# A half pair's transposes moved right behind the next scores, and LayerNorm work of each chunk moved from VectorE to ScalarE, in a two-layer graph kernel

## What is computed

```python
h = relu(layernorm(x))
g = exp0(log0(h) @ embed);  g = h_add(g, embed_bias)            # hyperbolic maps: norm, tanh, arctanh
neigh = exp0(adj @ log0(g))
x = x + h_add(exp0(log0(concat(h, neigh)) @ layer), layer_bias)
h = relu(layernorm(x))
for beta in (beta1, beta2):                                     # two attention layers
    n = h / norm(h)
    s = where(adj > 0, beta * (n @ n.T), -1e9)
    h = leaky(softmax(s) @ h, 0.3)
x = x + h
```

## Time and profile before

| | us |
|---|---|
| median of 3 runs (lowest to highest) | 994.92 (993.46 to 997.03) |
| profiled execution | 993.61 |
| its span | 992.1 |
| PE busy | 935.3 (94%) |
| DVE busy | 819.4 (83%) |
| ACT busy | 511.4 (52%) |

### The profile page before, as it was taken

One profiled execution on the slowest core, in us unless ns is written; L12 is line 12 of the kernel. 1 busy time (PEld: TensorE's weight loads), 2 busy tenths in 40 slices (PEclk: granted clock), 3 DMA queues, 4 the chain that ended last, 5 costly groups with the idle time before them and its releaser, 6 DMA issues.

```text
span 992.1 us, 22921 instructions
## 1 busy us (share of the span) xinstructions
PE 935.3 (94%) x9024; PEld 698.0 (70%) x9024; DVE 819.4 (83%) x2110; ACT 511.4 (52%) x708; POOL 8.0 (1%) x21
## 2 busy tenths in 40 slices
PE   2789999999997989999999999989999999999996
PEld 1754444444444878788888888768878888888885
DVE  7791888888888987788988898988768788888887
ACT  2720211211216575765656677777565565656564
POOL 0000000000000000000000000000000000000000
PEclk9879999999998999999999999999999999999999
DMA  8219888888881444555555655535655556555630
GB/s 343 94 62 312 278 284 277 278 286 298 275 275 43 168 174 177 207 210 219 211 200 195 244 206 192 183 145 187 238 183 212 211 193 245 213 204 205 252 139 36
DMA packets 29971, 207.26 MB, mean 209 GB/s; under 512 B 3632, under 2 KB 4272, under 8 KB 5296
## 3 DMA queue, kind: packets, MB, share of 16 engines
q1 hardware_dynamic: 28224, 203.44, 56.6%
q0 software_dynamic: 640, 2.10, 0.5%
q10 hardware_dynamic: 1008, 0.33, 0.1%
HBM read 203.75 MB, written 2.10 MB: 207 GB/s over the span
## 4 chain that ended last, share of the span: by engine, by line
PE 84%; DVE 8%; ACT 4%; issue 2%; DMA 1%; DVEq 0%; POOL 0%; SPq 0%; POOLq 0%; ACTq 0%
PE acc_ps L463 20%; PE s_ps L614 17%; PE s_ps L600 10%; PE acc_ps L667 6%; PE acc_ps L663 6%; PE acc_ps L665 6%; PE acc_ps L644 5%; PE acc_ps L640 5%; PE acc_ps L642 5%; PE acc_ps L427 1%; DVE work L1604 1%; ACT work L971 1%; DMA x_sb<-in_x 1%; ACT set L764 1%; PE s_ps L441 1%
## 5 line engine op out<-in xcount | busy, mean ns | idle before, releaser
L971 ACT ACTIVATE work<-s_ps,beta_bias,beta_scale 128x1024 f32<-128x1024 f32 x144 | 173.5, 1205 | 223.2 <-PE s_ps L614 223.2
L463 PE MATMUL acc_ps<-ring,set 128*128 128x512 f32 x512 | 225.6, 600 | 3.1 <-DVE set L1230 3.1
L1622 DVE SCALAR_TENSOR_TENSOR h_all<-ring,s_ps 128x1024 f32<-128x1024 f32 x112 | 136.6, 1220 | 69.9 <-PE s_ps L600 69.1
L463 PEld LDWEIGHTS acc_ps<-ring,set 128*128 128x128 f32 x512 | 97.3, 192 | 120.8 <-issue 117.8
L1604 DVE TENSOR_TENSOR work<-work 128x1024 f16<-128x1024 f32 x96 | 132.5, 1380 | 5.4 <-ACT work L981 5.4
L981 ACT ACTIVATE work<-work 128x1024 f16<-128x1024 f32 x96 | 131.5, 1369 | 3.1
L1612 DVE SCALAR_TENSOR_TENSOR work<-ring,work 128x1024 f32<-128x1024 f32 x96 | 116.7, 1215 | 0.0
L614 PE MATMUL s_ps<-xt 128*128 128x512 f16 x432 | 107.6, 385 | 6.3 <-ACT work L971 5.5
L614 PE MATMUL s_ps<-set 128*128 128x512 f16 x432 | 105.3, 379 | 2.6 <-ACT t L1029 2.1
L663 PE MATMUL acc_ps<-set,work 128*128 128x129 f16 x576 | 103.5, 220 | 4.6 <-DVE accs L1639 2.7
L663 PE MATMUL acc_ps<-src,work 128*128 128x129 f16 x576 | 102.9, 219 | 1.9 <-ACT accs L995 1.9
(11 more groups left out here) (254 smaller groups left out, 1726.1 us busy)
## 6 DMA issues: line engine op xcount, KB each, us to landing
ring<-in_adj_t SPq DMA_DIRECT2D x192, 1024.0 KB, 5.0
x_sb<-in_x SPq DMA_DIRECT2D x4, 512.0 KB, 7.3
out<-x_sb POOLq DMA_DIRECT2D x8, 256.0 KB, 2.5
w<-in_layer ACTq DMA_DIRECT2D x2, 64.0 KB, 8.7
w<-in_embed ACTq DMA_DIRECT2D x1, 64.0 KB, 4.2
eb<-in_embed_bias ACTq DMA_DIRECT2D x1, 64.0 KB, 7.0
lb<-in_layer_bias ACTq DMA_DIRECT2D x1, 64.0 KB, 11.3
beta<-in_beta ACTq DMA_DIRECT2D x2, 0.5 KB, 14.6
```

The costliest lines, as they stand in the source:

```text
L463: last = nc.tensor.matmul(agg, v_sb[:, jb, :], ring[:, k, b, :], start=jb == 0, stop=jb == NB - 1)
L971: nc.scalar.activation(values[x.n % VR], score_ps, ACT.Exp, bias=beta_bias[:, x.la:x.la + 1], scale=beta_scale[:, x.la:x.la + 1]).then_inc ...
L1622: V.scalar_tensor_tensor(turned[x.off % MR].rearrange("p (b j) -> p b j", b=CB), ring[:, x.mir_tile % AR, :, ds(x.h * HB * P, HB * P)], 0. ...
```

## The change

Five things. SP waits for all of `x` before the first tile of `adj`. ACT's separate ReLU pass goes: PE transposes the normalised rows and ACT applies ReLU while copying out; the one-column products stand in the loop, four behind each group. In the aggregation, the squares of the product, the ReLU after LayerNorm with its squares, and the scaled rows move from DVE to ACT, as in the last chunk. The last chunk has 12 pauses instead of 11. In `pairs`, the transposes of half n-1 stand right behind scores(n), the mirrored sum is that of n-2, and DVE's slot runs low halves(n-1), row total, own mask(n-2), mirrored mask(n-1).

```diff
             for i in range(XP):
                 sp.dma_start(x_sb[...]).then_inc(x_in[i], 16)
+            sp.wait_ge(x_in[XP - 1], 16)
...
-            relu(0)
             for r in range(NC):
-                if r + 1 < NC:
-                    relu(r + 1)
                 act.wait_ge(ht_done, r + 1)
-                nc.scalar.activation(ht_sb[:, ds(r * CH, CH)], ht_ps[r % 2], ACT.Copy).then_inc(ht_copied, 1)
+                nc.scalar.activation(ht_sb[:, ds(r * CH, CH)], ht_ps[r % 2], ACT.Relu).then_inc(ht_copied, 1)
...
             # ACT, gnn_chunk
                 on(ACT.Tanh, sm(5, CB), sm(4, CB))
+                chunk_squares(dump)
                 log_terms(sm(4, CB), sm(5, CB), sm(6, CB))
                 if not first and not c_last(c):
                     split_columns(0, c - 1, xt_ps)
                 on(ACT.Tanh, sm(5, CB), sm(4, CB))
-                on(ACT.Copy, x_sb[:, ds(c * CB, CB), :], t1[:, :, :])
+                chunk_relu(c, dump)
+                chunk_rows(c)
...
+            def chunk_relu(c, unused):
+                asked_for()
+                for b in range(CB):
+                    last = nc.scalar.activation(t2[:, b, :], t1[:, b, :], ACT.Relu, bias=small[:, 3, b:b + 1])
+                last.then_inc(chunk_made, 1)
+                act.wait_ge(chunk_made, c * 2 + 1)
+                for b in range(CB):
+                    last = nc.scalar.activation(unused[:, b, :], t2[:, b, :], ACT.Square, accum_out=...)
+                last.then_inc(told, 1)
+                nc.scalar.activation(x_sb[:, ds(c * CB, CB), :], t1[:, :, :], ACT.Copy)
+            def chunk_rows(c):
+                asked_for()
...
+                    last = nc.scalar.activation(t2[:, b, :], t2[:, b, :], ACT.Copy, scale=small[:, 1, b:b + 1])
...
+                    last = nc.scalar.activation(t3[:, b, :], t2[:, b, :], ACT.Copy, scale=small[:, 9, b:b + 1])
+                last.then_inc(xn_ready[0], 1)
+                nc.scalar.activation(src[0][:, ds(c * CB, CB), F:2 * F], t2[:, :, :], ACT.Copy, scale=FS)
...
             # ACT, last_chunk
                 pause(-1)
+                pause(0)
                 on(ACT.Tanh, sm(5, CB), sm(4, CB))
                 split_columns(0, c - 1, xt_before_ps)
-                pause(0)
                 pause(1)
...
             # ACT, slot
-                x = at(n - 4)
-                if x and x.off is not None and x.h == 1 and x.a == 0:
+                i, x = row_ending.get(n - 4), at(n - 3)
+                first = x and x.off is not None and x.h == 1 and x.a == 0
+                if i is not None and rows_of[i].a == 0:
+                    first_total(i)
+                elif first:
                     first_flush(x)
                 if at(n):
                     raise_scores(at(n))
-                i = row_ending.get(n - 4)
-                if i is not None and rows_of[i].a == 0:
-                    first_total(i)
...
             # PE, pairs
                     if at(n):
                         pair_scores(at(n))
-                    done, fresh = at(n - 3), at(n - 1)
-                    if done and done.off is not None:
-                        mirrored_sum(done)
+                    done, turned_last, fresh = at(n - 3), at(n - 2), at(n - 1)
+                    if fresh and fresh.off is not None:
+                        turns(fresh)
+                    if turned_last and turned_last.off is not None:
+                        mirrored_sum(turned_last)
                     if done:
                         own_sum(done)
...
                     if n in turned_at:
                         columns_turned(n)
-                    if fresh and fresh.off is not None:
-                        turns(fresh)
...
             # DVE, slot
-                x = at(n - 4)
+                x = at(n - 3)
                 if x and x.off is not None and x.h == 1 and x.a:
                     flush(x)
+                if at(n - 1):
+                    low_halves(at(n - 1))
+                i = row_ending.get(n - 4)
+                if i is not None:
+                    row_total(i)
                 x = at(n - 2)
+                if x:
+                    own_mask(x)
+                x = at(n - 1)
                 if x and x.off is not None:
                     mirrored_mask(x)
...
```

More of the change, by code:

```diff
@@ L188, in build @@
         xs_ready = sem("xs_ready")
-        h_ready = sem("h_ready")
         web_made = sem("web_made")
@@ L423, in _ @@
                 last.then_inc(g_done, 1)
-            pe.wait_ge(web_made, 1)
-            for b in range(NB):
-                last = nc.tensor.matmul(gb_ps[:, b:b + 1], ht_sb[:, ts(b, P)], web[:, :], start=True, stop=True)
-            last.then_inc(gb_done, 1)
+                if r == 0:
+                    pe.wait_ge(web_made, 1)
+                for b in blocks(r):
+                    last = nc.tensor.matmul(gb_ps[:, b:b + 1], ht_sb[:, ts(b, P)], web[:, :], start=True, stop=True)
+                last.then_inc(gb_done, 1)
             pe.wait_ge(weights_in, 16 * 5)
@@ L1052, in slot @@
                     raise_scores(at(n))
-                i = row_ending.get(n - 4)
-                if i is not None and rows_of[i].a == 0:
-                    first_total(i)
+                if i is not None and first:
+                    first_flush(x)
                 if at(n):
@@ L1254, in gnn_chunk @@
                 w_in = w_last_ps if c_last(c) else w_ps
-                rows = ds(c * CB, CB)
-                both, squares = slice(CB, 2 * CB), small[:, 2, 0:2 * CB]
                 dve.wait_ge(w_done, c + 1)
@@ L1262, in gnn_chunk, with chunk_product @@
                     split_columns(0, c - 1, xt_before_ps)
+                chunk_product(w_in, c)
+                chunk_bias(c)
+                chunk_norms(c)
+                atanh_over(sm(2, CB), sm(0, CB), sm(1, CB), CB)
+                if not first and not c_last(c):
+                    split_columns(0, c - 1, xt_ps)
+                product_scalars(small[:, 0, both], sm(2, CB), sm(9, CB), sm(10, CB), y2[:, 1:2], CB)
+                chunk_sum()
+                chunk_stats(c)
+                chunk_deviations()
+                chunk_scales()
+                chunk_low(c)
+            both, squares = slice(CB, 2 * CB), small[:, 2, 0:2 * CB]
+            def chunk_product(w_in, c):
                 answered()
@@ L1311, in gnn_chunk, with chunk_deviations @@
[L1311 removed]
+                ask(V.tensor_scalar(sm(3, CB), mean_var[:, 0:CB, 0], -1.0, None, ALU.mult))
+            def chunk_deviations():
+                answered()
                 step(V.tensor_scalar(squares, squares, TINY, None, ALU.max))
                 inv_sqrt(sm(1, 2 * CB), squares, sm(3, 2 * CB))
[L1314 to L1316 removed]
```

210 lines of the change are left out of this document (70 added, 140 removed).

## The result

The changed kernel takes 1052.0 us (median of 4 runs, 1051.5 to 1054.8) against 994.2 before: ratio 1.0582, 95% interval 1.0553 to 1.0611. It is 58 us slower; the forecast was 1046, with a range of 1008 to 1066. The profiled execution has a span of 1050.0 us.

A forecast was written before the change was run, and what follows sets the result against it. PE was taken to bound aggregation and pairs. Terms -2.1 + 17.3 + 2 + 3 + 36 - 3.8 - 1.5 + 1.8 (column transposes) gave +52.7 on 993.6 us: 1046 us, range 1008 to 1066.

The forecast's parts named there:

- What bounds the kernel: Aggregation and pairs: PE alone sets the end, so taking work off DVE or ACT there gives nothing.
- The start: Before the aggregation: DVE's wait for one-column products goes and ACT loses a pass; -2.1 us, ends -3.5 and -1.
- The chunk chain: Aggregation: sum copies behind ACT's chunk work lengthen the period from 29.7 to 32.5 us; +17.3, ends 0 and 24.
- The clock: Aggregation: PE's idle times before layer products may lower its clock; +2 us, ends 0 and 8.4.
- The passage: From chunks to pairs: one more stall, as the last sum's copies stand behind chunk 6's rows; +3 us, ends 0 and +6.
- The row stalls: Pairs, row starts: PE waits for low halves 1.37, then 1.14 us, and later in rows; +36 us, ends 22 and 46.
- Waits that go: Pairs: PE's two 1.9 us waits for ACT's total of row 0 vanish; -3.8 us.
- The layer boundary: Between layers: the 2.12 us wait and the 1.4 of clock behind it may go; -1.5 us, ends -6 and 0.
- the row stalls would be absorbed: Rival, pairs: low halves come sooner, so only the chunks' longer period costs; 1010 us, chance 0.10.
- the chunk chain covered: Rival, aggregation: halves between stretch ACT's times, so the period stays 29.7 and the transition as before; 1024 us, chance 0.12.
- The faster case: Rival, everywhere: DVE early enough; chunk's chain ends 26.7 us after product, low halves 4.2 after scores began; 984 us, chance 0.07.
- The case in which each stall costs clock: Rival, chunks and pairs: six chunk stalls cost 8.4 us instead of 2, half the 1.37 waits another 8; 1061, chance 0.09.

The follow-up runs named there:

- copies between: The changed kernel, but ACT copies the next chunk's sum between this chunk's ReLU and its scaled rows: 1032.5 us, ratio 1.0367.
- chunks-only: The changed kernel with the old order of the pairs put back on PE, ACT and DVE: 1019.2 us, ratio 1.0236.
- start, total, row 5: The kernel before with the changed start, row 0's total ahead of ACT's exponential, and row 5's columns one step later: 984.5 us, ratio 0.9906.
- start only: The kernel before with the changed start alone: 990.4 us, ratio 0.9945.

## Why the prediction was right, and where its terms were not

**What bounds the kernel** held. PE bounds both long stages; DVE's 28 us less gave PE nothing in the aggregation, where the stage with copies between was as long as before. In the changed kernel it is no longer true there: ACT's and DVE's chain sets the period.

**The start** was put at -2.1. The profile shows -3.3, its first product with `adj` varies from 58.1 to 62.5 us among kernels with the same start, and timed alone the start is worth 5 us of median (990.4 against 995.3), beyond the end of -3.5 that I gave. Over the ten kernels with the new start the mark is at 60.4 on average, over the two with the old one at 62.8. The sign held; how good the size was stays open.

**The chunk chain** was right. Predicted were copies 29.5 us behind a product; they start 28.6 to 30.9 behind it. Predicted was a spacing of 32.5; it is 32.8 where the clock stayed full. The chain alone, at about 18 us by the estimate above, is what the 17.3 counted (six times the 2.8 of its text would be 16.8). PE's waits, 14.0 us in six, come out smaller because slower matmuls used up part of them. The term that was mis-sized is the next one.

**The clock** was put at +2 with ends 0 and 8.4; by the estimate above it cost about 7.6 in the aggregation, near the far end. I took the low value since waits of up to 1.9 had left the clock alone, but the new ones were 2.0 to 2.9. The Trainium skill, "TensorE: Matmul & The Clock Gate", section "HAM oscillation — how this bites in real kernels", describes a loop in which every tile starts cold behind its wait. The waits of its example are about 3 to 5 us, longer than these six, so my "by that rule all six chunks pay" went further than the Trainium skill does. The trace has the fall behind four of six waits (two stretches at 0.66, two at 0.50); directly behind the two of 2.06 the clock was full.

**The passage** is the step that failed. I priced the late last product at +3, and the chunks-only run shows 3.7, though not by that product alone. I priced the new order of the pairs there at nothing, and it costs 11.6. DVE makes the last chunk's rows between these halves and is the late engine. Before, PE had its two sums to do while low halves were late, since the transposes stood behind them; now they stand behind the transposes that wait. The run with the own sum ahead of the transposes gave 5.7 us of that back, the one with the transposes last 6.8. So this explains about half; which part of the new order makes the other half was not separated. I had counted what stands behind the waiting instruction only for row starts.

**The row stalls** were right in mechanism and place: PE waits for low halves at the first and second mirrored half of a row, and a third time in layer 1. The sizes were 36 in the sum against 23.9 measured. That the waits list as a whole has 35.9, as I had said it would, is luck: 12.0 of it stand in the passage, where I had put none. The first was 1.11 instead of 1.37: PE arrived later, since it counts from the end of the scores (1.46 behind their start, not 1.29), and the low halves came 0.09 sooner. The second was 0.52 instead of 1.14. There I added the lengths of DVE's instructions, but they overlap: low halves, total, reciprocal and the two masks start 1.19, 0.72, 0.09, 1.12 and 1.13 us apart, and the low halves end 9.69 us after the scores instead of 10.2. The third was 0.95 instead of 1.45, and in layer 2 there was hardly any. Row 1 of either layer has no second wait, where 0.45 was counted.

**Waits that go**: the 3.8 us were exact. The layer boundary gives more than 1.5 where the rest of the order is left alone.

**The rivals.** That the row stalls would be absorbed, or the chunk chain covered, fell: both waits are there. The faster case fell by both its conditions, as counted. The case in which each stall costs clock was half right: its chunk part (8.4) is near what happened, but the row stalls cost no clock, which reads 1.00 in the rest of the kernel before and after.

So the total came out within 6 us by a sum in which one term was 12 too low and another 11 too high. The direction and the two main mechanisms were shown by the runs; the closeness of the total was luck.

## What to carry to other kernels

An instruction that may wait is placed by what stands behind it on its engine: the new order of the pairs, in which two sums stand behind transposes that wait, cost 32 us, and with the own sum ahead of them and the row total first 20 came back. Before work is moved to an idle engine, look at what that engine does next and who waits for it: two copies of half a microsecond made the aggregation 25 us longer when they stood behind the moved work, and 0.1 when they stood between its parts. And when removing one wait changes nothing, look for a second that the first was hiding, and try both edits together.

## What had not been expected

In the start PE ran the same matmuls at about half speed for a longer or shorter time in kernels with the same start, and the first product with `adj` came at 58.1 to 62.5 us. Busy time by stretch (columns as above), first of the changed kernel, then with chunks only, which has the same start:

```profile
24.00:29.00 5.00, 5.00 (x49) 5.00 (x48) 4.93 (x35) 4.89 (x22) 0.00 (x0) 1.00 1.01 426
```

```profile
24.00:29.00 5.00, 5.00 (x25) 5.00 (x26) 4.93 (x37) 2.57 (x11) 0.00 (x0) 1.00 1.01 424
```

49 matmuls in five microseconds against 25, while the granted clock reads 1.00 in both; the rows don't say why, and no run shows that the clock does it, as two of my expectations had it. In this stretch 49, 47, 32 and 25 matmuls ran in four kernels with the same start (the changed one; start, total, row 5; start only; chunks only), and their first products with `adj` came in the same order: 58.1, 58.9, 60.6 and 62.5. It scatters every comparison of the start by up to 4 us.

Two waits of 2.06 us left the granted clock full in the stretch directly behind them; those of 1.98, 2.13, 2.87 and 2.88 did not, nor did that of 2.12 in the kernel before. So the length of a wait alone does not decide it here. No run varied a wait by itself, and what decides stays open.
